# Sixteen sums on VectorE that pick each token's six expert weights, placed between the expert sets of batch 0

## The reference, cut to what matters

```
scores = sigmoid(logits) + gate_bias
...
topk_w, topk_i = lax.top_k(masked_scores, K)                 # K = 6
topk_w = topk_w / (topk_w.sum(axis=-1, keepdims=True) + 1e-08)
comb = zeros((T, E)).at[arange(T)[:, None], topk_i].add(topk_w)
h = silu(einsum('th,eih->eti', x, eg_w)) * einsum('th,eih->eti', x, eu_w)
routed = einsum('eti,ehi,te->th', h, ed_w, comb)
```

## Time and profile before

| | us |
|---|---|
| median of 3 runs | 1055.51 (1054.58 to 1059.43) |
| the profiled execution | 1065.52 |
| its span | 1063.8 |
| TensorE busy | 879.5 |
| VectorE busy | 726.7 |
| ScalarE busy | 565.1 |
| GpSimd busy | 252.4 |

### The profile page before, as it was taken

The page is one execution under the profiler, slowest core; times in us unless marked ns, Lnnn a source line. Parts: engine busy times, 40 slices in busy tenths (PEclk is TensorE's granted clock), DMA queues, the critical chain, the costliest instruction groups (busy, mean ns, idle before and its releaser), DMA issues. The chain is left out here.

```text
span 1063.8 us, 13432 instructions
## 1 busy us (share of the span) xinstructions
PE 879.5 (83%) x4333; PEld 453.7 (43%) x4333; DVE 726.7 (68%) x1323; ACT 565.1 (53%) x888; POOL 252.4 (24%) x348
## 2 busy tenths in 40 slices
PE   6899999999885527998999003869999999998998
PEld 3453344444222216887888001324433433343433
DVE  4879788888476576332655133679889888996675
ACT  3325666666762103553554001668769868875743
POOL 1011122222114777711770674000000000000000
PEclk9889899999986577998999555989999999998999
DMA  2732655642022124654774211100000020000001
GB/s 86 225 69 52 185 161 168 194 145 69 12 65 89 49 72 158 228 182 153 216 227 138 64 52 57 33 0 1 10 23 10 1 52 1 0 1 0 1 0 40
DMA packets 51054, 87.48 MB, mean 82 GB/s; under 512 B 11202, under 2 KB 22832, under 8 KB 49200
## 3 DMA queue, kind: packets, MB, share of 16 engines
q1 hardware_dynamic: 36716, 58.56, 18.6%
q10 hardware_dynamic: 8128, 15.47, 4.0%
q0 software_dynamic: 6144, 12.60, 3.7%
HBM read 43.28 MB, written 40.89 MB: 79 GB/s over the span
## 5 line engine op out<-in xcount | busy, mean ns | idle before, releaser
L1066 ACT ACTIVATE pt<-psum 128x1024 f32<-128x1024 f32 (+1 forms) x192 | 149.9, 814 | 115.6 <-PE psum L808 115.2
L1218 DVE TENSOR_REDUCE part_max<-psum 128x1 f32<-128x512 f32 (+3 forms) x304 | 184.5, 657 | 35.7 <-PE psum L790 19.9
L786 PE MATMUL psum<-ka,qa 72*128 72x512 bf16 (+3 forms) x384 | 115.1, 341 | 5.3 <-DVE part_max L1218 1.8
L746 POOL DMA_INDIRECT part<-slot_y,slot_row x96 | 92.9, 968 | 100.1 <-DMA slot_y<-pt 71.5
L735 POOL DMA_INDIRECT slot_x<-va,slot_row x96 | 95.4, 994 | 37.5 <-issue 29.0
L725 POOL TENSOR_SCALAR_AFFINE_SELECT pt<-pt 128x256 f32<-128x256 f32 x128 | 51.9, 407 | 220.0 <-ACT pt L1066 219.3
L808 PE MATMUL psum<-qa,ka 75*128 75x512 bf16 (+3 forms) x384 | 96.3, 334 | 3.1 <-DMA qa<-neg_t 1.5
L1426 DVE TENSOR_TENSOR moe_hid<-moe_silu,psum 128x256 f32<-128x256 f32 x56 | 23.3, 418 | 95.8 <-ACT moe_silu L1186 91.4
L824 PE MATMUL psum<-pt,va_g 128*32 128x512 f32 (+3 forms) x768 | 84.1, 511 | 0.4 <-POOL pt L725 0.3
L110 ACT ACTIVATE ln_sq<-psum 128x512 f32<-128x512 f32 x44 | 26.1, 594 | 100.4 <-PE psum L93 100.3
L786 PEld LDWEIGHTS psum<-ka,qa 72*128 72x128 bf16 x384 | 37.4, 98 | 81.1 <-DVE part_max L1218 59.6
(11 more groups left out here) (316 smaller groups left out, 1658.2 us busy)
## 6 DMA issues: line engine op xcount, KB each, us to landing
slot_x<-zero ACTq DMA_DIRECT2D x8, 1792.0 KB, 6.7
pt<-slot_x SPq DMA_DIRECT2D x56, 256.0 KB
slot_y<-pt SPq DMA_DIRECT2D x56, 256.0 KB, 2.1
qa<-in_moe_gu SPq DMA_DIRECT2D x4, 1024.0 KB, 5.8
qa<-rows_q SPq DMA_DIRECT2D x21, 192.0 KB
ka<-rows_k SPq DMA_DIRECT2D x21, 192.0 KB
wt_c<-in_channel_w SPq DMA_DIRECT2D x4, 576.0 KB, 4.0
o_den<-acc SPq DMA_DIRECT2D x32, 64.0 KB, 2.3
```

The source lines that it names most:

```text
L746: pool.indirect_dma_start(out=yg[:, n % 4, j, :], out_offset=None, in_=ys_d[b], in_offset=bass.IndirectOffsetOnAxis(ap=row[:, n, j:j + 1], ...
L786: mm = pe.matmul(bank[:, nk * h:nk * (h + 1)], qa[0:ROWS, g % RING, h0 + h, chunk(i, P)], ka[0:ROWS, g % RING, h0 + h, k0:k0 + nk], start= ...
L1066: act.activation(pt[:, u % 4, :, 0:n], score_bank[u % 2][:, :, 0:n], ACT.Exp, scale=SCALE)\
L1218: dve.tensor_reduce(part_max[:, h0:h0 + heads, slot], bank_of("fill", f)[:, 0:heads * nk].rearrange("p (h n) -> p h n", h=heads), AX_X, AL ...
```

## The change

The loop over `slot_weights` at the end of `after_attention` is gone. In batch 0, VectorE's step 1, 3, 5, ... 29 has one sum behind its product and its copy, and the sixteenth stands behind the last step of batch 0.

```diff
@@ after_attention (VectorE) @@
                     for c in range(NC):
                         shared_hidden(c)
                         add_shared(c)
-                    for n in range(NT):
-                        slot_weights(n)
 
                 def experts():
                     for b in range(B):
@@ experts (VectorE), for step in range(1, QUADS + 2) @@
                             if step <= QUADS:
                                 hidden(n - 1)
                             if step >= 2:
                                 keep_hidden(n - 2)
+                            if not b and step % 2:
+                                slot_weights(step // 2)
                             if b and step % 3 == 0 and 0 < step // 3 <= BLOCKS:
                                 combine(step // 3 - 1)
+                        if not b:
+                            slot_weights(NT - 1)
                     for n in range(BLOCKS, NT):
                         combine(n)
```

## The result

| | before | changed |
|---|---|---|
| median of 20 runs each, us | 1056.9 | 1048.35 |
| lowest to highest, us | 1051.06 to 1076.88 | 1044.04 to 1061.7 |
| profiled execution, us | 1065.52 | 1046.67 |
| its span, us | 1063.8 | 1045.0 |

The ratio of the runs, changed over before, is 0.992 with a 95% interval of 0.9896 to 0.9945: a gain of 8.5 us (5.8 to 11.0). The forecast was 10.5 us off the median, that is 1045.0 in a range of 1042.6 to 1049.6. The change makes the kernel faster.

A forecast was written before the change was run, and what follows sets the result against it. TensorE, busy 83% of the span, was taken to stall at the start of the sets behind VectorE's block of sums. 7.89 + 1.95 + 0.65 = 10.49 us off the median 1055.51 gave 1045.0 us, range 1042.6 to 1049.6.

The forecast's parts named there:

- Term 1: Start of batch 0's sets: TensorE's wait for the product of set 0 goes, 7.89 us gained.
- The terms are absolute times of a fixed stretch: Reason given for taking the summed gain of 10.49 us off the runs' median of 1055.51 us.
- Term 2: From turning of set 0 to rows of set 4: TensorE's clock stays up, 1.95 us gained (ends 0 and 1.95).
- Term 3: Scatters of batch 0 no longer lengthened beside sums, so loads and sets start 0.65 us earlier (ends 0 and 0.65).
- Cost among the sets: One sum of 1.78 us behind every second set's copy in batch 0 delays TensorE by 0.
- room of 3.94 us per sum: Between sets, a sum could grow from 1.78 to 3.94 us before TensorE waits.
- cost of either sign: TensorE's restart at batch 1 and the next stage: clock rise may win or lose 0.9 us; taken as 0.
- Loads, scatters of batch 1 and the two last sums: Around batch 0's sets and the start of batch 1: all were forecast to be in time, delaying nothing.
- the rows of set 4 are turned: Sign of being right: this comes 11.8 us after the first row load's issue, where it was 21.7.
- part of it is given back: Rival, chance 0.11: clock falls anyway or rows of sets 3 to 6 arrive late; 1047.6 or 1049.6 us.
- The fast end of the range: 1042.6 us, from 10.49 + 0.9 us and about 1 us for the runs' spread below their median.

The follow-up runs named there:

- fourteen in front: Changed kernel with fourteen sums in front of the sets and two between them: ratio 0.9945 against the kernel before.
- eleven: Changed kernel with eleven sums in front of the sets and five between them: ratio 0.9902 against the kernel before.
- kernel before with filled stall: Kernel before, sums still in front, with 32 useless 128 x 128 matmuls on TensorE in the stall: ratio 1.0021 against the kernel before.
- second trace of the kernel before: Kernel before, unchanged, run against itself and traced again: ratio 0.9982.
- these fillings: Kernel before with useless 128 x 128 matmuls on TensorE in the stall: 54 gave ratio 1.0041, 32 gave 1.0021.

## Why the prediction was right

- The bound, a stall of TensorE behind a block of VectorE, was the right one: with the sums gone from there the wait is gone, and part of it (fourteen in front) or all of it (eleven) goes with the number of sums that are taken out of the front.
- Term 1, 7.89 us, is the term that was mis-sized. The mechanism is right, the size is that of one execution: 7.89 us in one trace of the kernel before and 4.45 in the other. The step that failed is to take the duration of a wait, which is a difference of two chains, for a fixed time. "The terms are absolute times of a fixed stretch" was wrong for this one. That the sum of 10.49 us comes so near to the 10.8 us of the first trace is no test of the sizes, since the terms were read from that same trace.
- Term 2, 1.95 us for the clock: 5.55 against 3.38 in the changed kernel (395.48 to 398.86), 2.17 us, and 1.99 us in the kernel before with filled stall. It varies too: in the second trace of the kernel before the same piece takes 6.08 us (408.57 to 414.65), 2.70 us more than in the changed kernel, and there the lower clock also cost 1.1 us ahead of the stall (6.47 us at work from the first row turning to the stop, where the changed kernel needs 5.34 us up to the turning of set 0).
- Term 3, 0.65 us for the scatters: 0.61 us between the first traces, 0.61 to 0.88 over all.
- Cost among the sets: 0, measured 75.22 against 75.22 us. The room of 3.94 us per sum fits the rhythm (3.56 free, 5.34 not); its exact end was not measured. "It is 0 up to that length" was too broad: it does not hold in the last steps of a batch.
- The cost of either sign was there: 1.3 us in batch 1 between the first two traces, by an earlier rise of the clock. It is not the change's: the second trace of the kernel before has 153.30 as well.
- Loads, scatters of batch 1 and the two last sums did not become late, as said, and the rows of set 4 are turned 11.5 us after the first row load (forecast 11.8, before 21.7). One ground of the rival "part of it is given back" was misread: the row loads run on DMA queue q1 and the scatters on q0, so they do not share a queue.
- The fast end of the range does not come out of its sum: 1055.5 − 10.49 − 0.9 − 1 is 1043.1, not 1042.6. Nothing turns on it.

What stays open is the exact size. The landmarks of the stretch give 9.2 to 10.8 us, the three timed comparisons 8.5, 6.2 and 7.0. Each of their intervals holds 9.2, and only the first holds 10.8; weighted by their intervals they come to about 7.6 us (5.7 to 9.4, my estimate). So the gain is real, and nearer to 8 than to the forecast 10.5. That a part is given back later is not excluded. From the first scatter to the end of the span the two traces of the kernel before take 732.15 and 727.88 us and the changed kernel's three 720.64 to 720.90, a gain of 7.0 to 11.5 us. Behind the rows of set 4 it is 646.7 and 644.0 us before and 646.1 to 646.2 after: against the first trace nothing is given back, against the second 2.1 us, on average mostly in the stage of layer 1, where the code is the same (from the turning of the last combined tile to the end 409.4 to 412.0 us over the 14 traces). Two traces of the kernel before are too few to say whether that is chance. The time before the first scatter, the same code in all, strays from 321.5 to 339.0 us and may carry a part of it too; the timed runs have no trace, and I cannot show it.

## What to carry to other kernels

Work that nobody waits for yet belongs behind the first instruction that somebody waits for, not in front of it, on an engine that works in order; and how much fits between two such instructions is read from when the waiting engine wants the next one, not from the idle time of the engine that does the work. A wait in a trace is the difference of two chains: before it is booked as a gain, ask how long each chain takes in another run. When one stall is gone, look at once for the next instruction of the same engine that waits for a transfer in front of ready work.

## What the runs showed that I had not expected

- The code up to the first scatter is the same in all kernels and takes 321.5 to 339.0 us, in step with TensorE's clock before it (up to the first scatter 0.97 granted on average in the shortest, 0.92 in the longest). From one trace of each kernel a gain of 8 us can be read by landmarks only.
- A matmul of 128 x 128 numbers in f32 shows as two records and takes 0.226 us back to back at the full clock in these fillings (54 in 12.22 us), where a turning of the same shape takes 0.15 (four in 0.60 us).
- The clock does not fall at one fixed time after a stop. In the kernel before it fell 2.2 us after TensorE had stopped (0.94 granted between 405 and 406, the stop at 403.67), in its second trace 3.3 us after (0.85 granted between 406 and 408, the stop at 404.12), with fourteen sums in front 5.1 us after (the stop at 397.60, the fall at about 402.7), when TensorE had been at work again for 0.9 us.
